# Turning V by VectorE block transposes and on-chip transfers in an attention and gated-LoRA kernel

## What is computed

```python
q = (hidden_states @ wq.T).reshape(bsz, q_len, H, HD).transpose(0, 2, 1, 3)
k = (hidden_states @ wk.T).reshape(bsz, q_len, KV, HD).transpose(0, 2, 1, 3)
v = (hidden_states @ wv.T).reshape(bsz, q_len, KV, HD).transpose(0, 2, 1, 3)
...
probs = jax.nn.softmax(scores.astype(jnp.float32), axis=-1).astype(dt)
attn = jnp.einsum('bhqk,bhkd->bhqd', probs, v)
attn = attn.transpose(0, 2, 1, 3).reshape(bsz, q_len, H * HD)
return attn @ wo.T
```

## Time and profile before

| | us |
|---|---|
| median of 3 runs | 1325.56 (1325.34 to 1326.14) |
| the profiled execution, whole | 1326.35 |
| its span, first to last instruction | 1324.1 |
| TensorE's granted clock, mean of the span | 1.000 of full speed |
| VectorE, ScalarE, GpSimd busy | 960.1, 966.4, 427.5 |

### The profile page before, as it was taken

One profiled execution on the slowest core, in us unless ns is written; L12 is line 12 of the kernel. 1 busy time (PEld: TensorE's weight loads), 2 busy tenths in 40 slices (PEclk: granted clock), 3 DMA queues, 4 the chain that ended last, 5 costly groups with the idle time before them and its releaser, 6 DMA issues.

```text
span 1324.1 us, 22630 instructions
## 1 busy us (share of the span) xinstructions
PE 1302.2 (98%) x7000; PEld 1104.7 (83%) x7000; DVE 960.1 (73%) x2444; ACT 966.4 (73%) x2520; POOL 427.5 (32%) x345
## 2 busy tenths in 40 slices
PE   7899999999999999999999999999999999999998
PEld 6688788888888888888888888888888888888876
DVE  6976677777777677777767777767777767777776
ACT  5777577877778777778777777777677877776874
POOL 5413312423214332233414124141431433224323
PEclk9999999999999999999999999999999999999999
DMA  6000000201101000000000001000000100002124
GB/s 222 25 9 21 25 9 9 65 29 52 40 17 33 16 24 8 16 16 16 27 5 24 8 16 32 0 32 0 24 24 0 32 9 30 8 20 94 53 83 149
DMA packets 23530, 43.66 MB, mean 33 GB/s; under 512 B 2496, under 2 KB 2752, under 8 KB 23488
## 3 DMA queue, kind: packets, MB, share of 16 engines
q1 hardware_dynamic: 20896, 38.74, 9.5%
q10 hardware_dynamic: 2592, 4.40, 0.9%
HBM read 34.74 MB, written 8.39 MB: 33 GB/s over the span
## 4 chain that ended last, share of the span: by engine, by line
PE 91%; DVE 5%; ACT 1%; issue 1%; DMA 1%; POOL 1%; SPq 0%; DVEq 0%; ACTq 0%
PE bank_b L518 18%; PE bank_a L518 18%; PE bank_b L615 13%; PE o_ps L615 12%; PE pv_ps L608 10%; PE pair L592 7%; PE pair L599 6%; PE pair L588 2%; PE pair L590 1%; PE bank_a L578 1%; PE o_ps L518 1%; DMA x_sb<-x 1%; DVE pT_lo L1344 0%; DVE cosx L1318 0%; DVE probs L1355 0%
## 5 line engine op out<-in xcount | busy, mean ns | idle before, releaser
L403 POOL TENSOR_TENSOR rot<-rot,tab 128x512 f32<-128x512 f32 x160 | 206.9, 1295 | 594.0 <-ACT rot L920 593.7
L969 ACT ACTIVATE probs<-probs,row_min 128x128 f32<-128x128 f32 (+1 forms) x512 | 225.5, 447 | 1.0 <-DVE row_min L1355 0.8
L988 ACT ACTIVATE pT_hi<-pair 128x768 fp32r<-128x768 f32 x128 | 103.9, 812 | 165.7 <-PE pair L599 165.0
L980 ACT ACTIVATE probs<-probs,row_inv 128x128 f32<-128x128 f32 (+1 forms) x512 | 190.6, 445 | 22.1 <-DVE row_inv L1374 21.7
L1344 DVE TENSOR_TENSOR pT_lo<-pair,pT_hi 128x768 fp32r<-128x768 f32 x128 | 121.6, 950 | 86.1 <-ACT pT_hi L988 85.9
L386 POOL TENSOR_TENSOR w_hi<-raw,zero 128x512 fp32r<-128x512 f32 x74 | 84.9, 1147 | 241.7 <-PE bank_a L518 126.5
L518 PE MATMUL bank_a<-xT_hi,w_hi 128*128 (+1 forms) x376 | 149.9, 399 | 0.1
L518 PE MATMUL bank_b<-xT_hi,w_hi 128*128 (+1 forms) x376 | 149.8, 398 | 0.0
L518 PE MATMUL bank_a<-xT_hi,w_lo 128*128 (+1 forms) x376 | 146.8, 391 | 0.0
L518 PE MATMUL bank_b<-xT_hi,w_lo 128*128 (+1 forms) x376 | 146.8, 390 | 0.0
L518 PE MATMUL bank_a<-xT_lo,w_hi 128*128 (+1 forms) x376 | 146.3, 389 | 0.0
(11 more groups left out here) (182 smaller groups left out, 3274.3 us busy)
## 6 DMA issues: line engine op xcount, KB each, us to landing
raw<-w_seq SPq DMA_DIRECT2D x76, 256.0 KB, 2.6
gate_scratch<-b_raw ACTq DMA_DIRECT2D x16, 256.0 KB, 2.0
out<-y_sum SPq DMA_DIRECT2D x16, 256.0 KB, 2.0
x_sb<-x SPq DMA_DIRECT2D x3, 1024.0 KB, 11.0
mid<-x SPq DMA_DIRECT2D x7, 256.0 KB, 2.8
mid<-gate_scratch SPq DMA_DIRECT2D x7, 256.0 KB, 3.0
raw<-x SPq DMA_DIRECT2D x7, 256.0 KB, 2.6
raw<-gate_scratch SPq DMA_DIRECT2D x7, 256.0 KB, 3.0
```

Of the source, the lines that this page charges most:

```text
L403: nc.gpsimd.tensor_tensor(v, v, tab[:, s:s + SEQ].unsqueeze(1).to_broadcast([P, 2, SEQ]), ALU.mult).then_inc(sin_done[kind], 1)
L969: a = nc.scalar.activation(s, s, ACT.Exp, bias=row_min[:, j % 2, i:i + 1], scale=-1.0, accum_out=row_sum[:, i:i + 1])
L980: a = nc.scalar.activation(s, s, ACT.Copy, scale=row_inv[:, i:i + 1])
L988: nc.scalar.activation(pT_hi[:, :, :], pair[j % 2][:, :, 0:ROWS], ACT.Copy).then_inc(pThi_done, 1)
```

## The change

V of units 9 to 28 (made in units 8 to 27, for which `by_transfer(u)` holds) takes another way. VectorE transposes all 32x32 blocks of `bank_a` into `v_T` in one instruction. SP then issues sixteen transfers from SBUF to SBUF that put block (i, j) of the four tiles at block (j, i) of a new place `v_tok`, which is `b_raw`'s memory: each moves 32 partitions x 4 tiles x 32 floats, in runs of 128 bytes, 16 KB in all. ScalarE's `v_high` and VectorE's `v_low` read `v_tok` instead of `bank_a`. TensorE's four multiplications and ScalarE's `copy_vT` are left out in these units; TensorE's K projection waits for the block transpose instead. SP's loads of a group are put in another order around the moves, and its wait for the gate stores goes ahead of its loop. TensorE's and ScalarE's loops end at unit 27, with units 28 and 29 written out. V of the other 12 units is turned as before.

```diff
+MOVED = FINAL - WRITTEN
...
+        v_tok = b_raw
...
+        def by_transfer(u):
+
+            return not isinstance(u, int) or WRITTEN <= u < FINAL
+
+        def turned(u):
+
+            return u + 1 if u < FINAL else u + 1 - MOVED
...
+            def move_blocks(u):
+
+                sp.wait_ge(blocks_done, value(sp, u - WRITTEN + 1))
+                src = v_T[:, :].rearrange("p (t i b) -> p t i b", t=BLOCK_TILES, i=4)
+                dst = v_tok[:, :].rearrange("p (t d) -> p t d", t=BLOCK_TILES)
+                for i in range(4):
+                    for j in range(4):
+                        sp.dma_start(dst[32 * i:32 * i + 32, :, 32 * j:32 * j + 32],
+                                     src[32 * j:32 * j + 32, :, i, :]).then_inc(tok_in, 16)
+
             def group_chunks(g):
+
+                moved = not isinstance(g, int) or g >= WRITTEN // BLOCKS
+                u = lambda i: value(sp, BLOCKS * g + i)
+                g_next = value(sp, g + 1)
                 for c in range(WO + 2, CHUNKS):
                     load_chunk(g, c)
-                g_next = value(sp, g + 1)
-                for c in range(WO + 2):
+                load_chunk(g_next, WK)
+                load_chunk(g_next, WQ)
+                if moved:
+                    move_blocks(u(0))
+                    move_blocks(u(1))
+                for c in range(WQ + 1, WO):
                     load_chunk(g_next, c)
-
-            loop(sp, 0, KV_HEADS - 1, group_chunks)
+                if moved:
+                    move_blocks(u(2))
+                load_chunk(g_next, WO)
+                load_chunk(g_next, WO + 1)
+                if moved:
+                    move_blocks(u(3))
+
+            for g in range(WRITTEN // BLOCKS):
+                group_chunks(g)
+            for r in range(2):
+                sp.wait_ge(gate_out[r], 16 * TILES // 2)
+            loop(sp, WRITTEN // BLOCKS, KV_HEADS - 1, group_chunks)
...
@@ pe_unit @@
-                pe.wait_ge(vT_done, c2)
+                if not by_transfer(u):
+                    pe.wait_ge(vT_done, turned(u) + 1)
+                else:
+                    pe.wait_ge(blocks_done, value(pe, u - WRITTEN + 1))
                 project(K, bank_a, WK, x_2, w_2)
...
-                turn_v()
+                if not by_transfer(u):
+                    turn_v()
...
@@ PE and ScalarE programs @@
-            loop(pe, WRITTEN, LAST - 1, pe_unit)
+            loop(pe, WRITTEN, FINAL, pe_unit)
+            for u in range(FINAL, LAST - 1):
+                pe_unit(u)
...
+        def moved_high(moved, used):
+            nc.scalar.wait_ge(tok_in, moved)
+            nc.scalar.wait_ge(pv_done, used)
+            nc.scalar.activation(v_hi[:, :, :], v_tok[:, :].rearrange("p (k d) -> p k d", k=BLOCK_TILES),
+                                 ACT.Copy).then_inc(vhi_done, 1)
...
@@ act_unit @@
-                copy_vT(c2, c1)
+                if not by_transfer(u):
+                    copy_vT(c2, turned(u))
                 swap_halves(H3, bank_b, c2, H1, c2)
...
-                v_high(c2, n4[4])
+                if not by_transfer(u):
+                    v_high(turned(u) + 1, n4[4])
+                else:
+                    moved_high(value(nc.scalar, (u - WRITTEN + 1) * 256), n4[4])
                 exponents(1, n4[6])
...
+        def turn_blocks(count):
+
+            nc.vector.wait_ge(proj_done[V], count)
+            nc.vector.wait_ge(v_ready, value(nc.vector, count - 1))
+            nc.vector.transpose(v_T[:, :], bank_a[:, :]).then_inc(blocks_done, 1)
...
@@ dve_unit @@
             row_inverse(n4[4])
             dve_side(u, 2, 0)
+            if by_transfer(u):
+                turn_blocks(c2)
...
-                v_low(c2)
+                v_low(c2, v_tok if by_transfer(u) else bank_a)
```

More of the change, by code:

```diff
@@ L211, in build @@
         vT_done = sem("vT_done")
+        blocks_done = sem("blocks_done")
+        tok_in = sem("tok_in")
         vhi_done = sem("vhi_done")
@@ L321, in load_chunk @@
                 sp.dma_start(raw[:, c % 2, :], w_seq[value(sp, g * CHUNKS + c), :, :]).then_inc(raw_in[c % 2], 16)
+            def move_blocks(u):
[6 more added lines that the diff above has]
+                                     src[32 * j:32 * j + 32, :, i, :]).then_inc(tok_in, 16)
             def group_chunks(g):
+                moved = not isinstance(g, int) or g >= WRITTEN // BLOCKS
+                u = lambda i: value(sp, BLOCKS * g + i)
+                g_next = value(sp, g + 1)
                 for c in range(WO + 2, CHUNKS):
                     load_chunk(g, c)
-                g_next = value(sp, g + 1)
-                for c in range(WO + 2):
-                    load_chunk(g_next, c)
-            loop(sp, 0, KV_HEADS - 1, group_chunks)
+                load_chunk(g_next, WK)
[4 more added lines that the diff above has]
+                for c in range(WQ + 1, WO):
+                    load_chunk(g_next, c)
+                if moved:
[9 more added lines that the diff above has]
+            loop(sp, WRITTEN // BLOCKS, KV_HEADS - 1, group_chunks)
             for c in range(WO + 2, CHUNKS):
                 load_chunk(KV_HEADS - 1, c)
-            for r in range(2):
-                sp.wait_ge(gate_out[r], 16 * TILES // 2)
             def load_xg(t, s):
@@ L359, in _ @@
             sp.wait_ge(q_ready[K], UNITS)
-            sp.wait_ge(vt_ps, UNITS)
+            sp.wait_ge(vt_ps, UNITS - MOVED)
             load_xg(TILES - 2, 3)
@@ L1174, in _ @@
                 act_unit(u)
-            loop(act, WRITTEN, LAST - 1, act_unit)
+            loop(act, WRITTEN, FINAL, act_unit)
+            for u in range(FINAL, LAST - 1):
+                act_unit(u)
             act_unit(LAST - 1)
```

## The result

| | kernel before | changed kernel |
|---|---|---|
| median of the runs, us | 1325.85 | 1318.03 |
| profiled execution, us | 1326.35 | 1319.13 |
| its span, us | 1324.1 | 1316.9 |

The medians are of four runs each. Their ratio is 0.9936, with a 95% interval of 0.9924 to 0.9947, so the gain is small but clear of noise. The forecast was 1316.8 us.

What follows compares the result with a forecast made beforehand. TensorE's instruction list was taken to bound the loop; 20 units x 0.44 us for the turnings gave 8.8 us, all other terms nothing, so 1325.56 - 8.8 = 1316.8 us, range 1314.3 to 1327.5 us.

Steps and rivals of the forecast that it cites:

- What bounds the kernel: In the loop, TensorE's instruction list is the time (busy all of 790 us); the four turnings hold 0.44 us a unit.
- The sum: On TensorE, four multiplications fewer in each of 20 units: 20 x 0.44 = 8.8 us gained.
- ScalarE's copy, worth nothing: On ScalarE, removing 20 copies of 0.582 us gains nothing, since TensorE waits for no ScalarE result there.
- The block transpose: On VectorE between row_inverse and cosx: 0.69 us, bounds 0.4 and 1.4, no wait of TensorE's K projection.
- The transfers: SP's sixteen moves a unit: 9.4 us at 0.45 us an issue plus 2.6 us landing, early enough to cost nothing.
- T: Time from the first issue to the landing of the last of sixteen moves: taken as 9.4 us, from 7.0 to 17.1.
- sixteen issues within 7.5 us: Sign that the forecast is right: SP issues a unit's moves in that time, the last landing about 2.5 us behind.
- The packets, the other possible price: On the transfer engines: 144 packets per engine at 105 ns however small, 15.1 us, giving T = 17.1 us.
- The rule on small transfers: Skill page on the moves: 0.68 us at 4 KB, 0.95 at 64 KB; one after another, T = 12.8 to 16.9 us.
- The limit of T: At ScalarE's v_hi: moves cost nothing up to 14.0 us in 15 units, 12.6 us in a group's first units.
- Rival A: At ScalarE's v_hi in all 20 units: moves land late, at T = 17.1 us net 60 us slower, 1385.8; chance 0.15.
- Rival C: At TensorE's next scores: v_lo or VectorE's chain takes 0.4 us more, so no gain, 1325.6 us; chance 0.07.

Runs made afterwards that it cites:

- e1: Changed kernel with TensorE's four multiplications put back in units 8 to 27, their result unread: 1326.28 us, 1.0003 of the kernel before.
- e6: Changed kernel with VectorE's block transpose made three times, each after the one before ended: 1336.99 us, 1.0084 of the kernel before.
- e4: Changed kernel with each of the sixteen transfers cut to one tile, 32 runs, 4 KB: 1316.9 us in one execution.
- e7: Changed kernel with the sixteen transfers replaced by one to HBM and four back, 512 runs each: 1316.80 us, 0.9932 of the kernel before.
- e2: Changed kernel with 4 more transfers to an unused buffer ahead of the sixteen, ScalarE waiting for all: 1329.34 us, 1.0025 of the kernel before.
- e3: Changed kernel with 8 more transfers to an unused buffer ahead of the sixteen, ScalarE waiting for all: 1394.91 us, 1.0519 of the kernel before.
- e8: Changed kernel with V of units 29 to 31 also moved, by sixteen transfers each: 1321.20 us, 0.9962 of the kernel before.
- e9: Changed kernel with V of units 9 to 31 moved, each through HBM and four transfers back: 1317.97 us, 0.9937 of the kernel before.
- e10: The changed kernel run again, unaltered, beside the same runs of the kernel before: 1316.94 us, 0.9934 of the kernel before.

## Why the prediction was right

- **What bounds the kernel.** Right: PE was the time in the loop, and the chain's 0.44 us is what each unit lost and, in e1, got back. The sum said 8.8 us. The medians differ by 7.8 us in one comparison and 9.2 in the other (1326.14 - 1316.94), the ratios say 8.5 and 8.8, and twenty units took 9.0 and 9.3 us less.
- **ScalarE's copy, worth nothing.** Right as far as e1 shows: it is missing there and the time is the old one. `v_hi` from SBUF took 0.619 us against the 0.627 taken.
- **The block transpose.** 0.683 us (median of 20) against 0.69; TensorE never waited for it. In e6 it did, once 1.5 us were added to a slack forecast at 0.4 and 1.0 us; the forecast left out the 0.32 us from the transpose's end to TensorE's start, so the real slack is less.
- **The transfers.** The conclusion was right, the size was off: T was 11.5 us, not 9.4. The term that was too small is the issue, 0.64 us instead of 0.45, and the sign "sixteen issues within 7.5 us" failed with it: they took 10.3. The issue was taken from loads of as many runs, but runs are not what it goes by (e4, e7). The landing, 1.8 us, was shorter than the 2.6 taken. The packets, the other possible price, came to (0.122 x 1316.9 - 0.095 x 1324.1) x 16 / 46,080, about 12 ns each, not 105. So the margin in the first units was 1.0 us (0.4, and the 0.6 that ScalarE may be late), not the 3.2 forecast, and unit 8 used it up. That nothing was paid in the others is partly luck: 0.07 us more an issue (15 x 0.07 = 1.0) would have brought the waits of e2 on.
- **The rule on small transfers.** The Trainium skill, "DMA: Bandwidth & Descriptors", Bandwidth, gives 0.68 us for one transfer of 4 KB as the time that the engines are busy with it. The prediction's estimate of 12.8 us added fifteen such times one after another, which the page does not state. The traces do not bear that step out: all moves together kept the engines busy 0.122 x 1316.9 - 0.095 x 1324.1 = 34.9 us more, 0.11 us for each of 320. The pace was SP's 0.64 us, and that it lies near 0.68 is chance. Whether runs under 512 bytes are slowed, as its Specifications say, or are not from SBUF to SBUF, as its section "Why small descriptors are slow" says, no run here shows by itself.
- **The limit of T.** 12.6 and 14.0 us were forecast. With 4 more transfers T is 11.5 + 4 x 0.64 = 14.1, and TensorE waited 1.46 to 1.49 us in four of the first units and not in the others: the limits are about 12.6 and at least 14.1. Rival A lies beyond, and costs more than its formula: with T = 11.5 + 8 x 0.64 = 16.6 it gives 15 x 2.6 + 5 x 4.0 = 59 us, the waits alone were 56.5, but e3 lost 77, mostly through the clock.
- **Rival C**, a longer `v_lo`, did not come about in units 8 to 27, where it took 0.684 us (median) from SBUF as before from PSUM. When three more units were moved, it did in units 28 and 29, beside GpSimd's add (e8, e9).

## What to carry to other kernels

When one engine's instruction list is the time, count what leaves that list, and then ask of each replacement only how late it lands against the first engine that waits for it, in the tightest unit of the cycle and in the first pass of a loop. Here a chain of small transfers issued by one engine was as long as its issues, so it paid to make fewer of them (e7) and not to make them smaller (e4). Before work is moved from PSUM to SBUF operands, look at what GpSimd does at that moment (e9).

## What the runs showed that had not been expected

- An issue of a 32-partition transfer cost SP 0.59 to 0.63 us (medians) with 32, 128 or 512 runs, against 0.33 us for a 128-partition weight load of 128 runs. What in its form makes the difference was not tried.
- TensorE's granted clock fell from 1.00 to 0.62 and 0.53 after a wait of 4.03 us, for some 8 us (e3), and to 0.72 and 0.85 after one of 3.52 us in unit 8 of e2, while the waits of 1.46 us left the stretch from 700 to 1000 us of e2 at 1.00. Of e3's fifteen waits of about 2.3 us thirteen left it at 1.00; after the other two it was 0.50 for 2 us (from 992 and from 1164 us). A late transfer can therefore cost more than its lateness.
- The start varies from one execution to the next: TensorE's first turning of `x` into `o_ps` began at 57.0 us before, at 58.6 in the changed kernel's profile and at 55.7 in e10's, though e10's kernel is the same. That is most of the difference between their spans of 1316.9 and 1313.5 us. Without the start the spans are 8.8 and 9.3 us shorter than the one before.
